# Block attention's inputs: one set of moments for two normalisations, another order of the work, biases added elsewhere

## The reference

```python
y = (x - mean(x)) / sqrt(var(x) + 1e-5)
z = (y - mean(y)) * rsqrt(var(y) + 1e-5) * g + b
q, k, v = (z @ wq + bq) * 16 ** -0.5, z @ wk + bk, z @ wv + bv
o = softmax(q @ k.T) @ v          # by head
y = y + o @ wo + bo
```

## Time and profile before

| what | value |
|---|---|
| median of 3 runs | 953.02 us (952.41 to 955.83) |
| the profiled execution | 952.72 us, of which the span of the records is 950.9 |
| TensorE (PE) busy | 811.3 us, 85% of the span |
| VectorE (DVE) busy | 575.4 us, 61% |
| ScalarE (ACT) busy | 429.8 us, 45% |
| GpSimd (POOL) busy | 328.6 us, 35% |
| mean granted TensorE clock | 0.904 |
| p5 | 426.1 to 473.5 us |
| a1 | 473.5 to 519.0 us |

### The profile page before, as it was taken

How to read it: one execution, slowest core, us unless ns; L and a number is a source line. 1 busy time by engine, 2 the same in 40 slices (tenths; PEclk the granted TensorE clock), 3 DMA queues, 4 the chain that set the end, 5 groups by cost and what they waited for, 6 DMA issues and landing times. The chain is left out here.

```text
span 950.9 us, 20466 instructions
## 1 busy us (share of the span) xinstructions
PE 811.3 (85%) x7532; PEld 625.9 (66%) x7532; DVE 575.4 (61%) x1424; ACT 429.8 (45%) x1259; POOL 328.6 (35%) x463
## 2 busy tenths in 40 slices
PE   5999999798999999966977489999287886776997
PEld 4788887455999999843454478888166774464335
DVE  3564656436999999875395822232567775465473
ACT  2656666455655542023554300000268883754562
POOL 2111121022999999800042071100633432242001
PEclk9899999887999999975979579999679997988898
DMA  7011700000000000000000025552546310000001
GB/s 247 17 39 45 258 24 2 2 1 0 1 1 2 1 1 1 1 1 0 1 2 12 35 89 188 192 162 67 162 125 202 92 47 2 0 3 2 0 1 45
DMA packets 41847, 49.32 MB, mean 52 GB/s; under 512 B 7090, under 2 KB 37268, under 8 KB 41492
## 3 DMA queue, kind: packets, MB, share of 16 engines
q1 hardware_dynamic: 37204, 40.93, 13.4%
q0 software_dynamic: 1536, 4.20, 1.4%
q10 hardware_dynamic: 3008, 2.88, 0.9%
HBM read 43.81 MB, written 4.19 MB: 50 GB/s over the span
## 5 line engine op out<-in xcount | busy, mean ns | idle before, releaser
L723 POOL TENSOR_TENSOR r_faded<-r_state,rec_f 128x256 f32<-128x256 f32 x128 | 82.3, 644 | 20.1 <-DVE r_state L705 9.6
L751 PE MATMUL r_u_ps<-r_t_in,l_same_head 128*128 128x256 f32 x256 | 87.7, 425 | 0.0
L729 POOL TENSOR_TENSOR r_q_in<-r_state,rec_q 128x256 f32<-128x256 f32 x128 | 82.3, 643 | 0.3 <-DVE r_state L702 0.2
L758 PEld LDWEIGHTS r_o_ps<-l_head_of,r_q_in 128*128 128x128 f32 x512 | 77.0, 191 | 6.9 <-POOL r_q_in L729 0.4
L1088 ACT ACTIVATE a_prob<-a_s_ps,a_negmax 128x256 f32<-128x256 f32 x128 | 59.2, 486 | 20.8 <-DVE a_negmax L1144 20.8
L1431 ACT ACTIVATE a_prob<-a_s_ps,a_negmax 128x256 f32<-128x256 f32 x128 | 58.7, 485 | 17.0 <-DVE a_negmax L1469 17.0
L758 PE MATMUL r_o_ps<-l_head_of,r_q_in 128*128 128x8 f32 x512 | 65.0, 236 | 0.3 <-POOL r_q_in L729 0.3
L1667 POOL TENSOR_TENSOR a_prob<-a_prob,a_rden 128x512 f32<-128x512 f32 x32 | 32.4, 1043 | 84.2 <-DVE a_rden L1728 84.2
L1993 PE MATMUL m_h_ps<-m_rowsT,l_w 128*128 128x256 f32 x256 | 58.8, 390 | 0.0
L702 DVE TENSOR_TENSOR r_state<-r_update,r_faded 128x256 f32<-128x256 f32 x128 | 54.4, 425 | 4.4
L691 DVE TENSOR_TENSOR r_t_in<-r_state,r_par_ps 128x256 f32<-128x256 f32 x128 | 53.7, 421 | 5.3
(11 more groups left out here) (345 smaller groups left out, 1946.7 us busy)
## 6 DMA issues: line engine op xcount, KB each, us to landing
l_w<-in_B_w SPq DMA_DIRECT2D x16, 1024.0 KB, 5.6
a_ctxT<-in_ctxT SPq DMA_DIRECT2D x31, 256.0 KB, 2.7
a_ctx<-in_ctx SPq DMA_DIRECT2D x16, 256.0 KB
expert_out<-m_y ACTq DMA_DIRECT2D x7, 256.0 KB, 5.6
all_X<-in_x SPq DMA_DIRECT2D x4, 256.0 KB, 6.6
l_b<-in_B_b SPq DMA_DIRECT2D x1, 1024.0 KB
routed_rows<-ffn_xn SPq DMA_DIRECT2D x8, 128.0 KB, 1.8
l_F_up<-in_F_up SPq DMA_DIRECT2D x1, 1024.0 KB
```

The lines of the kernel that those rows point to most:

```text
L723: nc.gpsimd.tensor_tensor(faded[m][:, :, :], state[(t + 1) % 2][m][:, :, :], row("f", t, m), ALU.mult).then_inc(faded_ready[m], 1)
L729: nc.gpsimd.tensor_tensor(q_in[t % 2][m][:, :, :], state[t % 2][m][:, :, :], row("q", t, m), ALU.mult).then_inc(q_ready[m], 1)
L751: nc.tensor.matmul(u_ps[t % 2][m][:, 0:B, :], same_head[:, :], t_in[m][:, :, :], start=False, stop=True).then_inc(u_mm[m], 1)
L758: mm = nc.tensor.matmul(o_ps[:, 2 * m + c, :, t % U], q_in[t % 2][m][:, c * (B // 2):(c + 1) * (B // 2), :], head_of[:, :], start=True, st ...
```

## The change

In p5 there is one `Normed` of X, whose root has another scale and epsilon (eps2) so that it gives z's normalisation directly; Y's root and reciprocal are made once for all tiles, and Y's rows are written late on VectorE, before the last keys. Values copies are shared: ScalarE takes one sequence of a tile (two copies), VectorE the other (two). The zero fill is in two halves and waits for the first two scaled tiles. TensorE's order puts turns and values products of the second half between wide products of the first. The products with one row are gone: bv is added in a1 when the heads are copied (two ScalarE operations with a bias, in place of one copy), and bo is added to Y by GpSimd at the start of a1, eight additions of 128x256, for which VectorE's `add` waits. B_bo is loaded broadcast to all partitions.

```diff
-def attention_inputs_stage(nc, stage, X, Y, eps, ident, xnT, gain, shift, wq, bq, wk, bk, wv, bv, ones, par, QT, keys, vblk):
+def attention_inputs_stage(nc, stage, X, Y, eps, ident, xnT, gain, shift, wq, bq, wk, bk, wv, par, QT, keys, vblk):
     N = 512
     with Scope(nc, stage) as sc:
-        first = Normed(nc, sc, "x", X, eps, keep=Y)
-        second = Normed(nc, sc, "y", Y, eps, ident, xnT, gain, shift)
+        normed = Normed(nc, sc, "z", X, eps, ident, xnT, gain, shift)
+        eps2 = sc.sb("eps2", [P, 1])
+        y_std, y_rstd = (sc.sb(n, [P, NT]) for n in ("y_std", "y_rstd"))
         y_ps = [sc.ps(f"y_ps{j}", [P, 2, D]) for j in range(2)]
         qk_ps = [sc.ps(f"qk_ps{j}", [P, N]) for j in range(4)]
-        zeroed, y_mm, y_taken, k_mm, k_taken, q_mm, q_taken = (sc.sem(n) for n in ("zeroed", "y_mm", "y_taken", "k_mm", "k_taken", "q_mm", "q_taken"))
+        zeroed, eps2_ready, y_std_ready, y_rstd_ready, y_mm, y_taken, y_taken_too, k_mm, k_taken, q_mm, q_taken = (sc.sem(n) for n in (
+            "zeroed", "eps2_ready", "y_std_ready", "y_rstd_ready", "y_mm", "y_taken", "y_taken_too", "k_mm", "k_taken", "q_mm", "q_taken"))
+        def values_of(t, b):
+            for e in range(2):
+                yield (vblk[e * T:(e + 1) * T, 2 * t + b, :, e * HD:(e + 1) * HD],
+                       y_ps[t % 2][b * T:(b + 1) * T, 0, :].rearrange("p (h e d) -> p h e d", h=HH, e=2)[:, :, e, :])
         with sc.block() as block:
             @block.gpsimd
             def _(pool):
-                nc.gpsimd.memset(vblk[:, :, :, :], 0.0).then_inc(zeroed, 1)
+                nc.gpsimd.memset(eps2[:, :], EPS * EPS).then_inc(eps2_ready, 1)
+                pool.wait_ge(normed.scaled, ONE + 2)
+                for i in range(2):
+                    nc.gpsimd.memset(vblk[:, i * (B // 2):(i + 1) * (B // 2), :, :], 0.0).then_inc(zeroed, 1)
             @block.vector
             def _(dve):
@@ -561,91 +577,132 @@
                                                       bk[:, m:m + 1], par[:, e:e + 1], ALU.add, ALU.mult)
                     ins.then_inc(k_taken, 1)
+                def take_values(t):
+                    dve.wait_ge(y_taken, ONE + t + 1)
+                    for out, values in values_of(t, 1):
+                        ins = nc.vector.tensor_copy(out, values)
+                    ins.then_inc(y_taken_too, 1)
+                def rows(t):
+                    nc.vector.tensor_scalar(Y[:, t, :], X[:, t, :], normed.meanvar[:, t, 0:1], y_rstd[:, t:t + 1], ALU.subtract, ALU.mult)
                 for g in range(NT // 2 + 1):
                     if g < NT // 2:
-                        first.moments(dve, 2 * g)
-                        first.moments(dve, 2 * g + 1)
+                        normed.moments(dve, 2 * g)
+                        normed.moments(dve, 2 * g + 1)
                     if g >= 1:
-                        dve.wait_ge(first.scaled, ONE + 2 * g)
-                        second.moments(dve, 2 * g - 2)
-                        second.moments(dve, 2 * g - 1)
+                        normed.inverses(dve, g - 1)
                     if g < NT // 2:
-                        first.variances(dve, g)
+                        normed.variances(dve, g)
                     if g >= 1:
-                        second.variances(dve, g - 1)
-                    if g < NT // 2:
-                        first.inverses(dve, g)
-                        first.scale(dve, 2 * g)
-                        first.scale(dve, 2 * g + 1)
-                    if g >= 1:
-                        second.inverses(dve, g - 1)
-                        second.scale(dve, 2 * g - 2)
-                        second.scale(dve, 2 * g - 1)
-                for c in range(2):
-                    for m in range(KD):
-                        take_keys(c, m)
+                        normed.scale(dve, 2 * g - 2)
+                        normed.scale(dve, 2 * g - 1)
+                    if g >= 3:
+                        take_values(g - 3)
+                for t in range(2, 4):
+                    take_values(t)
+                for m in range(KD):
+                    take_keys(0, m)
+                for t in range(4, NT):
+                    take_values(t)
+                dve.wait_ge(y_std_ready, ONE + 1)
+                nc.vector.reciprocal(y_rstd[:, :], y_std[:, :]).then_inc(y_rstd_ready, 1)
+                dve.wait_ge(y_rstd_ready, ONE + 1)
+                for t in range(NT):
+                    rows(t)
+                for m in range(KD):
+                    take_keys(1, m)
             @block.tensor
             def _(pe):
                 def values(t):
-                    pe.wait_ge(second.taken, ONE + t + 1)
+                    pe.wait_ge(normed.taken, ONE + t + 1)
                     if t >= 2:
-                        pe.wait_ge(y_taken, ONE + t - 1)
+                        pe.wait_ge(y_taken_too, ONE + t - 1)
                     for k in range(KD):
-                        nc.tensor.matmul(y_ps[t % 2][:, 0, :], xnT[:, k, t * P:(t + 1) * P], wv[:, k, :], start=(k == 0), stop=False)
-                    nc.tensor.matmul(y_ps[t % 2][:, 0, :], ones[0:1, :], bv[0:1, :], start=False, stop=True).then_inc(y_mm, 1)
+                        mm = nc.tensor.matmul(y_ps[t % 2][:, 0, :], xnT[:, k, t * P:(t + 1) * P], wv[:, k, :], start=(k == 0), stop=(k == KD - 1))
+                    mm.then_inc(y_mm, 1)
                 def channels(c, m, w, acc, done, taken):
+                    pe.wait_ge(normed.taken, ONE + 4 * c + 4)
                     if c >= 1:
                         pe.wait_ge(taken, ONE + KD * (c - 1) + m + 1)
                     for k in range(KD):
                         mm = nc.tensor.matmul(acc[:, :], w[:, k, m * P:(m + 1) * P], xnT[:, k, c * N:(c + 1) * N], start=(k == 0), stop=(k == KD - 1))
                     mm.then_inc(done, 1)
-                for c in range(2):
-                    for t in range(4 * c, 4 * c + 4):
-                        second.turn(pe, t)
-                        if t >= 1:
-                            values(t - 1)
-                    if c == 1:
-                        values(NT - 1)
-                    pe.wait_ge(second.taken, ONE + 4 * c + 4)
-                    for m in range(KD):
-                        channels(c, m, wk, qk_ps[m], k_mm, k_taken)
-                        channels(c, m, wq, qk_ps[2 + m], q_mm, q_taken)
+                def key_channels(c, m):
+                    channels(c, m, wk, qk_ps[m], k_mm, k_taken)
+                def query_channels(c, m):
+                    channels(c, m, wq, qk_ps[2 + m], q_mm, q_taken)
+                for t in range(4):
+                    normed.turn(pe, t)
+                    if t >= 1:
+                        values(t - 1)
+                normed.turn(pe, 4)
+                values(3)
+                normed.turn(pe, 5)
+                key_channels(0, 0)
+                values(4)
+                normed.turn(pe, 6)
+                key_channels(0, 1)
+                values(5)
+                normed.turn(pe, 7)
+                query_channels(0, 0)
+                values(6)
+                query_channels(0, 1)
+                values(7)
+                for m in range(KD):
+                    key_channels(1, m)
+                for m in range(KD):
+                    query_channels(1, m)
             @block.scalar
             def _(act):
+                def roots(g):
+                    act.wait_ge(normed.var_ready, ONE + 2 * g + 2)
+                    nc.scalar.activation(normed.std[:, 2 * g:2 * g + 2], normed.meanvar[:, 2 * g:2 * g + 2, 1], ACT.Sqrt, bias=eps2[:, 0:1], scale=1.0 + EPS).then_inc(normed.std_ready, 1)
                 def take_values(t):
                     act.wait_ge(y_mm, ONE + t + 1)
-                    if t == 0:
-                        act.wait_ge(zeroed, ONE + 1)
-                    for b in range(2):
-                        for e in range(2):
-                            ins = nc.scalar.activation(vblk[e * T:(e + 1) * T, 2 * t + b, :, e * HD:(e + 1) * HD],
-                                                       y_ps[t % 2][b * T:(b + 1) * T, 0, :].rearrange("p (h e d) -> p h e d", h=HH, e=2)[:, :, e, :], ACT.Copy)
+                    act.wait_ge(zeroed, ONE + t // 4 + 1)
+                    for out, values in values_of(t, 0):
+                        ins = nc.scalar.activation(out, values, ACT.Copy)
                     ins.then_inc(y_taken, 1)
                 def take_queries(c, m):
                     act.wait_ge(q_mm, ONE + KD * c + m + 1)
                     nc.scalar.activation(QT[:, m, c * N:(c + 1) * N], qk_ps[2 + m][:, :], ACT.Identity, bias=bq[:, m:m + 1]).then_inc(q_taken, 1)
-                first.roots(act, 0)
-                first.roots(act, 1)
-                second.roots(act, 0)
-                for c in range(2):
-                    for t in range(4 * c, 4 * c + 4):
-                        if t % 2 == 0 and t // 2 + 2 < NT // 2:
```

(64 more changed lines are left out.)

10 lines of the change are left out of this document (5 added, 5 removed).

## The result

The changed kernel takes 928.21 us, the median of 4 runs (925.47 to 929.64), against 952.71 of the kernel before: a ratio of 0.976 (95% interval 0.9722 to 0.9798), 24.5 us faster, below the range given. A later comparison gave 927.04 against 947.16, a ratio of 0.979 (0.9773 to 0.9808), 20.1 us. The kernel before took 947.13 to 947.52 us in all three later comparisons, each on another chip, so the 952.71 of the first is the figure that stands apart, and 20.1 us is the better one for the gain. The profiled execution has 928.02 us and a span of 925.6.

A forecast was written before the change was run, and what follows sets the result against it. VectorE's normalisation chain was taken to bound p5 until 433.4, TensorE from there, and VectorE the first units of a1. Gains of 14.1 us in p5 and 2.7 in a1 summed to 16.8, giving 936, range 931.5 to 943.

The forecast's parts named there:

- p5: Stage making the block attention's inputs, 426.1 to 473.5 (47.4 us) before the change; forecast gain 14.1 us.
- a1: Attention stage, 473.5 to 519 before the change; gain 2.7 us forecast from fewer one-row products and a vanished VectorE wait.
- all stages beside p5 and a1: Rest of the kernel: given no gain, the whole forecast saving being 14.1 plus 2.7 us.
- The start: Beginning of p5: first transposition near 428.7, 4.7 us earlier; tile 2's values product at 435.0, between 434.8 and 435.9.
- the prediction's case for a pair caught by both: Start of p5: second scale pair blocked by both zero-fill halves would end near 433.2, against 430.5 without a lock.
- I take 441: p5: TensorE's clock rises to full at 441, costing 0.65 us beyond 439.7, so TensorE ends at 458.5.
- the stage without one-row products: Stage before p5: products began at about 414, full clock from 418; its some 3.5 us put p5's rise at 438.5 to 440.2.
- early clock: Rival for p5: work from 430 counts, full clock from 435, ScalarE then bounds some tiles; 933.5 us, chance 0.15.
- the 8 us that didn't lift the clock: Argument against an early rise: in the old p5, similar work with one-row products between left the clock at half.
- the rival that keeps only them: First transposition no earlier, only one-row products go: 6.6 us in p5, 2.7 in a1; about 943, chance 0.10.
- ScalarE as the next bound: p5, values 2 to turn 5 after an early full clock: ScalarE's take and two copies need some 1.5 us a tile.
- the earliest case: Fastest total considered: full clock in p5 from 435, giving 933.5 us, at a chance of 0.15.

## Why the prediction was wrong

The sign and most of the mechanism were right: an earlier start, an earlier full clock, fewer products. 936 was forecast, in 931.5 to 943, and 928.21 came. Two terms of the sum failed. The time of the clock's rise was put too late, which is 3.0 us. And all stages beside p5 and a1 were put at nothing, where this pair of executions has 0.5 us ahead of p5 and 5.0 behind a1. The 17.0 + 2.8 = 19.8 us of the two stages alone would have put the profiled execution at 952.7 - 19.8 = 932.9, inside the range, and the gain of the later comparison, 20.1 us, is 3.3 above the 16.8 forecast.

- **The start:** right. Transposition 2.2 us into the stage (2.6 forecast); values 2 at 434.73 in a stage that began at 425.62, 9.1 us in (8.9 forecast). The second scale pair was held by both halves of the fill and ended at 432.0, 6.4 us in; the prediction's case for a pair caught by both, 433.2, was 7.1 in. It ended sooner because one scale came through behind each half. Of what that cost, one profile with the fill moved shows 0.9 us on the path, and the times of the two kernels show no difference. The rule of the Trainium skill (SBUF — State Buffer, "SBUF: two separate sides") that one instruction holds the shared port for its whole length agrees with the 3.11 us here and the 1.53 and 0.70 with the fill moved, but for the 0.15 us by which each held scale ended behind its half, less than the 0.4 of a free one.
- **The clock: the step that failed.** "I take 441" put the rise 14.9 us into the stage; it came at 434, 8.4 us in. The rest of the difference follows from that: values 2 to turn 5 took 434.73 to 437.26 = 2.5 us instead of 4.6, and there was no 0.65 behind them; what followed took 455.06 - 437.26 = 17.8 against 18.1. That is 2.1 + 0.65 + 0.3 = 3.0 us, and with the start 0.2 later it is p5's whole miss (17.0 against 14.1). The miss came of two choices: the work before 435 was left out of the count, and 441 was set between 438.5 to 440.2, from the stage without one-row products, and 444.9, from the stage with them. The rival *early clock* had it right, full clock from 435 and 933.5 us, at a chance of 0.15. What spoke against it in the text, the 8 us that didn't lift the clock, were cycles with one-row products in them, and the stage without them had lifted it. With the one-row products put back, TensorE was busy 10.90 of 10.90 us and stayed at 0.50; with the same products at 128 rows the clock was full 8.5 us into the stage. The Trainium skill (TensorE: Matmul & The Clock Gate, "What's actually happening") says that activity releases the half clock; the changed kernel agrees (full at 434), and the 10.90 us at 0.50 are a case which the busy time alone would have got wrong.
- **The price of the one-row products in p5** was put at their own time, 6.6 us in the rival that keeps only them. Moving the biases alone gave 8.6 us in the whole, 7.4 of it in p5 even with ScalarE as the new bound; putting them back into the changed kernel's p5 cost 11.6 us in p5 in its one, long execution, and some 10 in the whole by the medians (938.05 against 928.21). About half of the 11.6 is clock: from values 2 at 437.95 to about 449.4 TensorE worked at half of the full rate, an estimated 5.7 us. The rest is the products' own time.
- **ScalarE as the next bound** was named only for the early clock, at 1.5 us a tile. With the old four copies it is 1.8, and the shared copies were costed at nothing though they are worth some 1.2 us once the clock is full, an estimate from the 2.0 us of waits with four copies and the 0.8 with two. VectorE's copy was 0.29 each (0.27 taken).
- **a1:** right. 2.8 measured, 2.7 forecast. The wait of 0.67 is gone; the heads' pair cost 0.83, not 1.02; GpSimd's additions 5.50, not 5.8, and hidden by 1.95.
- **The 5 us behind a1** were put at nothing, and they are the larger part of the miss. Most of them are of this pair of executions and not of the change: the same program gave 431.9 and 427.5 there, and in the later comparison, without them, the ratio was 0.979. That is bad luck for the number, not a fault of the working on p5 and a1. The lower end of the range, 931.5, lay 2.0 us below the earliest case, the only room for such shifts; one profile can't show that they are larger.

Taken apart, in single profiles, p5 goes from 47.4 us to 40.0 without the one-row products, to 40.4 with the one set of moments and shared copies alone, to 31.8 with both, and to 30.4 with the new order. The 7.4 and 7.0 of the single parts add to 14.4; together they gave 15.6.

## What to carry to other kernels

Read the granted clock beside each kind of product, not beside TensorE's busy share: before costing a change to a stage that runs at half clock, compare what stands in it with the nearest stage where the clock did rise, and test the difference in content as the cause. In this kernel a bias added by a one-row product cost more than its columns; adding it elsewhere, or giving the product 128 rows, took that cost away. Once a stage's clock doubles, look at which engine paces it then: here copies that were free at half clock were the bound at full clock. And before the stages that a change doesn't touch are put at nothing, profile the kernel before twice: here they moved by 4 us.

## What the runs showed of the hardware

- With one-row fp32 products of 256 columns (two instructions each) among the 128-row work, the granted clock stayed at 0.50 until 22 us into a stage in which TensorE waited only 0.47 us behind its first turn (one profile, of an execution 5 us above the kernel's median); with the same products at 128 rows, mostly zeros, it rose 8.5 us in. In the kernel before the same padding brought the rise from 25.6 us into the stage to 15.1.
- At full clock the one-row pair takes 0.62 us to the next product, the 128-row pair 0.43; at half clock 1.15 and 0.85 (429.05 to 429.90).
- In a3 of the kernel before, TensorE pauses 1.25 and 1.53 us in two profiles inside one group of scores, with no semaphore to wait for. The pause is there in all four profiles of programs with 7532 TensorE instructions (1.26 us with 128-row products, 0.94 with the one-row products and the old order back in the changed kernel), at another product in both with 7516 (0.90 and 1.15 us, the two with bv in p5), and in none of the six with 7500. So it goes with the program and not with the execution; what causes it is open, since no run changed the number of instructions alone.
